# Two self-attentions of a decoder rebuilt around 32-row heads in fp32

## The chip, the cores and the metric

One core of a Trainium2 chip runs the whole program. The metric is the device time of one execution in microseconds (us); less is better. TensorE (PE) multiplies matrices, VectorE (DVE), ScalarE (ACT) and GpSimd (POOL) do elementwise work, and SyncE (SP) issues most DMAs. Results of TensorE land in PSUM, eight banks of 128 partitions by 512 fp32 numbers.

## What is computed

A decoder of four layers (attention, cross attention, feed-forward, each followed by a layer norm) on x of 2 x 1024 x 256. The change touches two of its attentions, both with 16 heads of width 16:

```python
# layer 1: causal
q = split_heads(x @ Wq + bq); k = split_heads(x @ Wk + bk); v = split_heads(x @ Wv + bv)
scores = einsum('bhqd,bhkd->bhqk', q, k) / sqrt(16)
scores = where(tril, scores, -10000.0)
ctx = softmax(scores) @ v;  return merge(ctx) @ Wo + bo
# layer 3: the last 64 keys, no biases
valid = (kpos >= qpos - 64 + 1) & (kpos <= qpos)
scores = einsum('bhqd,bhkd->bhqk', q, k) / sqrt(16) + where(valid, 0, -inf)
out = softmax(scores) @ v;  return merge(out) @ Wo.T
```

## The kernel before, in words

The stages run one after the other, each in blocks that end with all engines meeting. `attention` (line 775) makes the causal stage L1a and the window stage L3a. The 16 heads are cut into 4 units of 4 heads (HU = 4), for each of the 2 sequences: 8 units, in which every stage loops.

Each unit has two products of queries and keys. A **piece** has queries on the partitions and up to 512 keys in a row (`max_ps`, line 959), and VectorE takes its row maximum (`cmax`, line 1104). When a unit's 48 pieces (32 in the window stage) are done, VectorE negates and joins the maxima (`negc`), TensorE transposes them (`turn`, line 978), VectorE copies them (`crow`) and GpSimd's queue moves them by a DMA into one more row of the queries (line 938), so that the second product already has the maximum taken off. The **scores** (`st_ps`, line 997) have the keys on the partitions and up to 512 queries in a row; ScalarE takes exp of two heads at once (`prob`, line 1093). Then `values` multiplies prob by V with a column of ones (`acc`, line 1022); four heads go to four groups of 32 columns of the array. VectorE transposes acc, takes the reciprocal of the sums, multiplies, and transposes back into `o` (lines 1127 to 1141).

To be precise enough on TensorE's fp32r path, which takes one pass where fp32 takes two records of two passes each, the kernel splits queries and keys into a high and a low part. `project` makes them for all heads (lines 1034 and 1037), ScalarE writes the high part (line 1084), VectorE the low part (line 1164), SP stores them to memory (line 884) and loads them back four times stacked (lines 902, 907 and 910) as `qst` and `kst`, with 4 x 16 rows and one for the maximum. GpSimd first clears these buffers (lines 927 to 934). Masks are added by a second matmul with an identity (`identb`, lines 963, 966, 1000, 1003), for both products.

The order on TensorE is written out by hand: in the opening, all projections, with the first unit's pieces between the last of them; then per unit and step (12 in the causal stage, 8 tiles of 192 queries cut at the half in the window stage) scores of heads 0 and 1, scores of heads 2 and 3, and `values` of the step before, with the next unit's pieces dealt out at four spots of the step. Three banks hold pieces, so the next piece waits for the reduce of three pieces ago.

Two other stages serve the prediction as measures. `cross_attention` (line 1200) already keeps its heads in 32 rows each, of which 17 are used, in plain fp32 (line 1328 scores, line 1349 values, line 1291 projection). `paired_attention` (line 1507, stage L2a) runs two heads at a time in 64 rows each (line 1687 pieces, line 1701 scores, line 1716 values), with 16 steps per unit and three piece banks.

Of the kernel before, what the change touches and what calls it, by code (L numbers as in the profile page):

```python
# [5 lines left out]
F32 = mybir.dt.float32  # L6
# [29 lines left out]
STAGES = 7  # L36
# [723 lines left out]
def max_pieces(kind):  # L760

    out = []
    for t in range(S // P):
        if kind in ("full", "causal"):
            keys = S if kind == "full" else (t + 1) * P
            out += [(t, h, 1, k, min(CH, keys - k), k // CH) for h in range(HU) for k in range(0, keys, CH)]
        elif kind == "window":
            first = max(0, t * P - WIN)
            out += [(t, h, 2, first, (t + 1) * P - first, 0) for h in range(0, HU, 2)]
        else:  # L770
            out.append((t, 0, HU, 0, M, 0))
    return out


def attention(nc, env, dram, kind, scale, w_count, mask=None, ahead=None, masks=None):

    cross = kind in ("cross", "xcausal", "xmask")
    nk = M if cross else S
    nkp = M + 1 if cross else S
    kp = M if cross else P
    nkt = 1 if cross else S // P
    halves = S // CH
    steps = [(half, i == 0, i == len(steps_of(kind, half)) - 1, *t)
             for half in range(halves) for i, t in enumerate(steps_of(kind, half))]
    nsteps = len(steps)
    pieces = max_pieces(kind)  # L790
    NP = max(p[5] for p in pieces) + 1
    per_unit = len(pieces) + 1
    units = [(b, u) for b in range(NB) for u in range(NU)]
    piece_steps = {"full": range(0, nsteps - 1), "causal": range(0, nsteps - 2),
                   "window": range(2, nsteps - 3)}.get(kind, range(0, 2))
    turn_step = piece_steps[-1] + 1

    def pieces_at(i, spot):

        if i not in piece_steps:  # L800
            return range(0)
        n, i = 4 * len(piece_steps), 4 * piece_steps.index(i) + spot
        return range(i * len(pieces) // n, (i + 1) * len(pieces) // n)

    MAXB = 3
    RING = 4
    SLOTS = 4 if cross else 3
    LEAD = 2 if cross else 1
    items = []
    for b in range(NB):  # L810
        for m in range(KT):
            items += [(b, "q", m, c * CH, CH) for c in range(S // CH)]
# [2066 lines left out]
```

## Time and profile before

| | |
|---|---|
| median of 3 runs | 3301.66 us (3295.03 to 3303.44) |
| the profiled execution | 3299.8 us, span of its trace 3298.0 us |
| mean granted TensorE clock | 0.868 of 2.4 GHz |
| busy: PE, DVE, ACT, POOL | 2587.0, 1677.4, 1081.4, 759.1 us |
| costliest groups of L1a and L3a | reduce of pieces 268.6 us (line 1104), exp 211.7 (line 1093), matmuls of pieces 225.4 (line 959) and scores 203.1 (line 997), values 185.0 (line 1022) |

The busy sum of a group is the time in which at least one of its instructions runs; where four row tiles of the array work at once it is less than count times mean. Fp32 matmuls stand as two records each. A matmul's start is measured, its end modelled, so a cost per matmul is best read from one start to the next.

### The profile page before, as it was taken

Reading aid. Unit: us, or ns where it says so; the run is one execution under the profiler, and the core shown is the slowest. Engines: PE = TensorE matmul, PEld = TensorE weight load, DVE = VectorE, ACT = ScalarE, POOL = GpSimd, SP = SyncE. Lnnn points to the kernel's source line nnn. Section 1 sums busy time; section 2 is a strip of 40 time slices with the busy share of each in tenths; the row PEclk is TensorE's granted clock in tenths of the full one; section 3 lists DMA queues with packets and bytes.
Section 4 is the critical chain, followed back from the end, with each engine's and each line's share of the span. In section 5 each row is a group of like instructions: output and inputs, shape, how many; then the busy total and the mean of one; then the engine's idle time right before and its main releaser. Section 6 shows DMA issues by size and latency. Waiting matters only on the chain. (4 is left out here: it accounts for less than half of the span.)

```text
span 3298.0 us, 38083 instructions
## 1 busy us (share of the span) xinstructions
PE 2587.0 (78%) x14160; PEld 1667.8 (51%) x14160; DVE 1677.4 (51%) x3198; ACT 1081.4 (33%) x1858; POOL 759.1 (23%) x596
## 2 busy tenths in 40 slices
PE   0153089799999889996799898858889989589992
PEld 0143076444444357994333333336657753379992
DVE  6716963556645532224688874545635554441115
ACT  4212023234344321111165657331313333214441
POOL 7385903100000101332200000003140021025551
PEclk9956589899999889997898979868989999669996
DMA  3012103642300022994311110004186410139994
GB/s 129 15 62 87 53 1 84 112 52 33 46 1 21 2 103 71 332 332 145 58 20 29 30 20 7 2 10 129 44 183 79 53 36 2 50 131 353 353 346 184
DMA packets 92689, 313.41 MB, mean 95 GB/s; under 512 B 21279, under 2 KB 39991, under 8 KB 74194
## 3 DMA queue, kind: packets, MB, share of 16 engines
q1 hardware_dynamic: 76442, 276.93, 29.7%
q0 software_dynamic: 16064, 34.04, 3.3%
q8 instruction: 114, 1.87, 0.2%
q14 instruction: 69, 0.57, 0.1%
HBM read 258.74 MB, written 38.61 MB: 90 GB/s over the span
## 5 line engine op out<-in xcount | busy, mean ns | idle before, releaser
L1104 DVE TENSOR_REDUCE cmax<-max_ps 128x1 f32<-128x512 f32 (+5 forms) x512 | 268.6, 549 | 176.9 <-PE max_ps L963 71.2
L1808 DVE TENSOR_REDUCE cmax<-max_ps 128x1 f32<-128x512 f32 x512 | 318.6, 682 | 71.9 <-PE max_ps L1687 71.9
L1093 ACT ACTIVATE prob<-st_ps 128x1024 f32<-128x1024 f32 (+3 forms) x336 | 211.7, 652 | 372.4 <-PE st_ps L1000 171.4
L2428 PE MATMUL A<-xbT,w 128*128 128x128 f32 x2512 | 301.7, 276 | 2.3 <-DMA w<-L3f_W_dram 1.9
L2428 PEld LDWEIGHTS A<-xbT,w 128*128 128x128 f32 x2512 | 291.5, 193 | 3.4 <-DMA w<-L3f_W_dram 2.4
L1784 ACT ACTIVATE prob<-st_ps 128x1024 f32<-128x1024 f32 x256 | 247.1, 1021 | 140.2 <-PE st_ps L1701 140.2
L959 PE MATMUL max_ps<-kst,qst 128*128 128x192 f32 (+4 forms) x640 | 225.4, 397 | 25.2 <-DVE cmax L1104 13.1
L1687 PE MATMUL max_ps<-kst,qst 48*128 48x512 f32 x512 | 203.3, 504 | 41.1 <-DVE cmax L1808 21.0
L2439 PE MATMUL C<-w,hid 128*128 128x256 f32 x944 | 223.0, 380 | 0.0
L997 PE MATMUL st_ps<-qst,kst 128*128 128x512 f32 (+5 forms) x672 | 203.1, 378 | 20.1 <-DMA qst<-crow 17.4
L959 PEld LDWEIGHTS max_ps<-kst,qst 128*128 128x128 f32 x640 | 128.7, 205 | 143.0 <-DVE cmax L1104 102.5
L1687 PEld LDWEIGHTS max_ps<-kst,qst 48*128 48x128 f32 x512 | 88.3, 204 | 220.3 <-DVE cmax L1808 195.0
L2618 DVE COPY yb<-C 128x256 f32<-128x256 f32 x118 | 50.1, 424 | 283.4 <-PE C L2439 283.4
L2343 POOL DMA_INDIRECT y_rows_dram<-yb,dst x118 | 116.3, 986 | 330.5 <-DVE yb L2618 327.3
L1022 PE MATMUL acc<-prob,v 128*17 128x512 f32 (+5 forms) x1344 | 185.0, 419 | 0.7
L2439 PEld LDWEIGHTS C<-w,hid 128*128 128x128 f32 x944 | 170.6, 191 | 18.3
L2332 POOL DMA_INDIRECT xb<-x_rows_dram,src x118 | 115.4, 978 | 173.7 <-DVE dst L2593 138.4
L997 PEld LDWEIGHTS st_ps<-qst,kst 128*128 128x128 f32 x672 | 132.9, 206 | 41.6 <-DMA qst<-crow 20.1
L1716 PE MATMUL acc<-prob,v 128*17 128x512 f32 x1024 | 151.2, 666 | 0.4 <-ACT prob L1784 0.4
L1701 PE MATMUL st_ps<-qst,kst 49*128 49x512 f32 x512 | 140.2, 458 | 2.7 <-ACT prob L1784 2.7
L938 POOL DMA_DIRECT2D qst<-crow x16 | 8.4, 527 | 547.5 <-DVE crow L1118 547.5
L2499 ACT ACTIVATE hid<-A,w 128x128 f32<-128x128 f32 x316 | 90.1, 368 | 114.1 <-PE A L2428 114.1
(403 smaller groups left out, 4857.7 us busy)
## 6 DMA issues: line engine op xcount, KB each, us to landing
w<-L3f_W_dram SPq DMA_DIRECT2D x79, 1026.0 KB, 8.4
w<-L1f_W_dram SPq DMA_DIRECT2D x39, 1536.0 KB, 9.3
qst<-q_parts_dram SPq DMA_DIRECT2D x64, 256.0 KB, 9.5
kst<-k_parts_dram SPq DMA_DIRECT2D x64, 256.0 KB, 15.7
down_coef<-L0f_down_coef_dram SPq DMA_DIRECT2D x10, 1024.0 KB, 4.8
coef_u<-L0f_up_coef_dram SPq DMA_DIRECT2D x10, 1024.0 KB, 4.6
gate<-L2f_gates_dram SPq DMA_DIRECT2D x6, 1536.0 KB, 8.2
q_parts_dram<-o SPq DMA_DIRECT2D x16, 512.0 KB, 9.7
```

Of the source, the lines that this page charges most:

```text
L959: mm = pe.matmul(max_ps[:, g % MAXB, at:at + ne], qst[:, gu % SLOTS, h + a, t * P:(t + 1) * P], kst[:, gu % SLOTS, h + a, k0:k0 + ne], sta ...
L997: mm = pe.matmul(out, kst[:, gu % SLOTS, h, j * P:j * P + kp], qst[:, gu % SLOTS, h, lo:hi], start=True, stop=(not masked), skip_group_che ...
L1022: mm = pe.matmul(acc[32 * a:32 * a + HD + 1, lo - half * CH:hi - half * CH], v[:, b, j, u * HU + a, :], prob[:, g % 2, a, 0:hi - lo], star ...
L1093: act.activation(prob[:, g % 2, 2 * p:2 * p + 2, 0:hi - lo], st_ps[0:kp, p, :, 0:hi - lo], ACT.Exp, scale=scale).then_inc(s.exp_done, 1)
L1104: dve.tensor_reduce(cmax[:, h:h + nh, t, part], max_ps[:, g % MAXB, :].rearrange("p (a n) -> p a n", a=nh)[:, :, 0:n], AX.X, ALU.max).then ...
L1687: mm = pe.matmul(max_ps[:, e % MAXB, at:at + ne], qst[rows, gu % SLOTS, p, t * P:(t + 1) * P], kst[rows, gu % SLOTS, p, k0:k0 + ne], start ...
L1701: mm = pe.matmul(st_ps[0:kp, p, side, 0:hi - lo], kst[rows, gu % SLOTS, p, j * P:j * P + kp], qst[rows, gu % SLOTS, p, lo:hi], start=True, ...
L1716: mm = pe.matmul(acc[32 * a:32 * a + HD + 1, lo - half * CH:hi - half * CH], v[:, b, j, u * HU + a, :], prob[:, g % 2, a, 0:hi - lo], star ...
L1784: act.activation(prob[:, g % 2, 2 * p:2 * p + 2, 0:hi - lo], st_ps[0:kp, p, :, 0:hi - lo], ACT.Exp, scale=scale).then_inc(s.exp_done, 1)
L1808: dve.tensor_reduce(cmax[:, first:first + len(pairs), tiles[0]:tiles[0] + len(tiles), part], max_ps[:, e % MAXB, :].rearrange("p (a c n) - ...
L2428: mm = pe.matmul(A[:, j % 2 * 2 + a, f * TB:(f + 1) * TB], up_w(w[:, j % WB], a, k, f), xbT[:, j % 2, k, :], start=(k == 0), stop=(k == KT ...
L2439: mm = pe.matmul(C[:, j % 2, 0:D], hid[:, j % 2, f, 0:TB], down_w(w[:, j % WB], f), start=(f == 0), stop=(f == NF - 1))
```

## The change

Both stages go from `attention` to a new `self_attention`.

- Queries and keys are projected per unit and half of the sequence, in plain fp32, straight into `qT` and `kT`, in which head a of a unit has rows 32a to 32a+15 and row 32a+16 is the maximum (in kT a one). The weights come padded from the host and are loaded ahead, in the norm of the stage before (`more` and `w3`, two DMAs where there were three). The split into parts, the stores, the loads and the clearing are gone. Each unit has its own 4 projections (64 matmuls in all, as large as the 32 of before).
- The projections and V are no longer made in the opening, apart from the first unit's: they are dealt out after steps (`projections_due`).
- A **group** of matmuls takes scores of two heads and pieces of the two others, each in its own 32 rows. A step is group 0, `weigh` (the values) of two steps ago, group 1, and what is due. `weigh` issues its four heads without pieces between them.
- One ring of three PSUM banks serves pieces, turns, projections and V, in one order.
- The scores have no mask matmuls; GpSimd zeroes the masked part of prob with `affine_select` (line 932 of the new file), and `weigh` waits for that. The pieces keep theirs.
- Pieces lead by a whole unit (12 or 4 chunks), the maxima are turned per half unit, and SP issues four small DMAs for each turn. prob has three buffers.
- In the window stage a step joins two or three tiles of queries (4 steps per unit), a chunk two, and one reduce serves two tiles.

The core of the diff, new code only (in `group`, p is the group and c the chunk of pieces one unit ahead):

```python
                def group(step, p, c):
                    if pack:
                        g = step // nS
                        if step:
                            pe.wait_ge(s.exp_done, 2 * (step - 1) + p + 1)
                        if p == 0 and opens[step % nS]:
                            pe.wait_ge(c_loaded[half_of[step % nS]], 16 * HU * (g + 1))
...
                    for i in range(max(len(pack), len(chunk))):
                        if i < len(pack):
                            j, lo, hi, at = pack[i]
                            for side in range(2):
                                a = 2 * p + side
                                rows = slice(32 * a, 32 * a + HD + 1)
                                mm = pe.matmul(st_ps[:, p, side, at:at + hi - lo], kT[rows, g % SLOTS, j * P:(j + 1) * P],
                                               qT[rows, g % SLOTS, lo:hi], start=(i == 0), stop=True, skip_group_check=True)
...
                        if i < len(chunk):
                            t, k0, k1, at = chunk[i]
                            for side in range(2):
                                a = 2 * (1 - p) + side
                                key = ("piece", c, a)
                                if i == 0:
                                    room(key)
                                rows = slice(32 * a, 32 * a + HD)
                                mm = pe.matmul(spot(key)[:, at:at + k1 - k0], qT[rows, gm % SLOTS, t * P:(t + 1) * P],
                                               kT[rows, gm % SLOTS, k0:k1], start=(i == 0), stop=(not masked), skip_group_check=True)
...
                for step in range(NS):
                    c = step + LEAD if step + LEAD < NC else None
                    group(step, 0, c)
                    if step >= LAG:
                        weigh(step - LAG)
                    group(step, 1, c)
                    if c is not None:
                        extras(c)
```

`room(key)` waits until the holder of three ring entries ago is read. `extras` is the turn, if one is due, then the projections due: in the causal stage after chunks 0, 2, 4 and 7 of 12, in the window stage after 0 (two of them), 1 and 2 of 4.

```python
                for step in range(NS):
                    for i, (sign, base, c0, c1) in enumerate(masked_sides(step)):
                        if i:
                            pool.wait_ge(s.cleaned, cleaned_by[step] + i)
                        else:
                            pool.wait_ge(s.exp_done, 2 * (step + 1))
                        to = prob[:, step % PROBS, :, c0:c1]
                        pool.affine_select(out=to, in_=to, compare_op=ALU.is_ge, fill=0.0, base=base,
                                           pattern=[[0, HU], [sign, c1 - c0]], channel_multiplier=-sign).then_inc(s.cleaned, 1)
```

TensorE at the start of stage L1a, before: all projections (`w_1` are the weights; 1034 queries, 1037 keys, 1040 V), then the first pieces.

```order
L1034 MATMUL st_ps<-xT,w_1 128x512 x4
L1037 MATMUL st_ps<-xT,w_1 128x512 x4
L1034 MATMUL st_ps<-xT,w_1 128x512 x4
L1037 MATMUL st_ps<-xT,w_1 128x512 x4
L1040 MATMUL st_ps<-w_1,xT 128x256 x16
L1034 MATMUL st_ps<-xT,w_1 128x512 x4
L1037 MATMUL st_ps<-xT,w_1 128x512 x4
L1034 MATMUL st_ps<-xT,w_1 128x512 x4
L1037 MATMUL st_ps<-xT,w_1 128x512 x2
L959 MATMUL max_ps<-kst,qst 128x128
```

The same place now (952 is a projection of keys by `more` or queries by `w_1`, 962 of V, 998 pieces, 1006 their mask).

```order
L952 MATMUL ring<-xT,more 128x512 x2
L952 MATMUL ring<-xT,w_1 128x512 x2
L952 MATMUL ring<-xT,more 128x512 x2
L952 MATMUL ring<-xT,w_1 128x512 x2
L998 MATMUL ring<-kT,qT 128x512 x2
L1006 MATMUL ring<-causal_qk,identb 128x128 x2
L998 MATMUL ring<-kT,qT 128x512 x2
L1006 MATMUL ring<-causal_qk,identb 128x128 x2
L952 MATMUL ring<-xT,more 128x512 x2
L962 MATMUL ring<-w_1,xT 128x256 x4
```

The first piece now comes after 8 projecting matmuls and none of them has a trip through memory behind it; the rest of the projections has moved between the chunks.

TensorE in the middle of a causal unit, one step of 512 queries without a causal mask on the scores, before.

```order
L997 MATMUL st_ps<-qst,kst 128x512 x2
L959 MATMUL max_ps<-kst,qst 128x512
L997 MATMUL st_ps<-qst,kst 128x512 x2
L959 MATMUL max_ps<-kst,qst 128x256
L963 MATMUL max_ps<-causal_qk,identb 128x128
L1022 MATMUL acc<-prob,v 17x512 x2
L959 MATMUL max_ps<-kst,qst 128x512
L1022 MATMUL acc<-prob,v 17x512 x2
L959 MATMUL max_ps<-kst,qst 128x256
L963 MATMUL max_ps<-causal_qk,identb 128x128
```

And now (986 scores, 1045 the values in `weigh`), one step and the next one's start.

```order
L986 MATMUL st_ps<-qT,kT 128x512 x2
L998 MATMUL ring<-kT,qT 128x512 x2
L1045 MATMUL acc<-prob,v 17x512 x4
L986 MATMUL st_ps<-qT,kT 128x512 x2
L998 MATMUL ring<-kT,qT 128x512 x2
L986 MATMUL st_ps<-qT,kT 128x512 x2
L998 MATMUL ring<-kT,qT 128x512 x2
L1045 MATMUL acc<-prob,v 17x512 x4
```

Scores and pieces alternate in pairs, the values have become one run of four, and group 1 of a step stands right ahead of group 0 of the next.

GpSimd in the window stage, before: it clears the three slots of queries and keys, then issues a DMA per unit.

```order
L931 MEMSET kst 128x4096
L932 MEMSET qst 128x4096
L934 MEMSET kst 1x4096
L931 MEMSET kst 128x4096
L932 MEMSET qst 128x4096
```

And now: small clears, then the masking of prob, 17 instructions per unit (14 of 4 heads x 128 columns, 3 of 4 x 64).

```order
L921 MEMSET v 128x256
L922 MEMSET cmax 128x32
L932 AFFINE_SELECT prob<-prob 128x4x128 x7
L932 AFFINE_SELECT prob<-prob 128x4x64 x2
L932 AFFINE_SELECT prob<-prob 128x4x128 x7
L932 AFFINE_SELECT prob<-prob 128x4x64
```

The big clears of the opening have gone, and GpSimd works inside every step; in the causal stage it has 8 such instructions per unit, all of 4 x 128.

## Rows read from the trace of the kernel before

**Rows 1.** Windows: us, busy per engine (count), granted clock, DMA share, GB/s.

```profile
545.00:627.00 82.00, 63.22 (x209) 36.32 (x209) 41.58 (x83) 12.28 (x17) 40.76 (x15) 0.87 0.90 187
627.00:962.00 335.00, 322.46 (x1806) 156.07 (x1806) 204.71 (x398) 131.46 (x169) 13.50 (x21) 0.98 0.26 33
2390.00:2452.00 62.00, 53.97 (x193) 32.52 (x193) 26.72 (x51) 12.28 (x17) 38.64 (x14) 0.90 0.85 175
2452.00:2480.00 28.00, 22.57 (x116) 16.33 (x116) 5.72 (x11) 4.26 (x10) 0.59 (x1) 0.53 0.74 152
```

**Rows 2.** Timeline: start, length, engine, line; L1a's first matmul, first scores, first after it; L3a's end.

```profile
545.47 1.19 PE L1034 MATMUL st_ps<-xT,w 128*128 128x512 f32 x1 [1.77 <-PEq L2752]
...
627.34 0.79 PE L997 MATMUL st_ps<-qst,kst 128*128 128x512 f32 x1 [4.00 <-DMA qst<-crow]
...
989.18 3.39 PE L1193 MATMUL y_ps<-wo,o 128*128 128x256 f32 x8 [2.60 <-PEq L828]
...
2637.74 4.52 PE L1193 MATMUL y_ps<-wo,o 128*128 128x256 f32 x12 [2.60 <-PEq L828]
```

**Rows 3.** Sources: the DMA of each unit's maxima in L1a, in L3a, and L3a's first projections.

```profile
L938 POOL DMA_DIRECT2D qst<-crow x8: 501/507/766, 624.3 to 958.8; - x8
L938 POOL DMA_DIRECT2D qst<-crow x8: 496/497/591, 2452.1 to 2619.5; - x8
L1034 PE MATMUL st_ps<-xT,w x32: 592/592/1193, 2390.1 to 2423.6; 128*128 128x512 f32 x32
```

**Rows 4.** Timeline of TensorE in cross attention, clock 1.00: values, scores, projection; then a mask.

```profile
1062.64 1.05 PE L1349 MATMUL acc<-prob,v 77*17 77x512 f32 x8
1063.62 1.10 PE L1328 MATMUL st_ps<-qT,kT 17*77 17x512 f32 x8
1064.65 1.98 PE L1291 MATMUL pr_ps<-xT,wx 128*128 128x512 f32 x4
1066.47 2.56 PE L1307 MATMUL max_ps<-kbd,qT 128*128 128x308 f32 x8
...
1070.97 0.42 PE L1334 MATMUL st_ps<-causal_kq,identb 128*77 128x128 bf16 x4
1071.22 1.94 PE L1291 MATMUL pr_ps<-xT,wx 128*128 128x512 f32 x4
```

**Rows 5.** Timeline of TensorE in L1a: values in two halves, then in one run.

```profile
803.54 1.04 PE L1022 MATMUL acc<-prob,v 128*17 128x512 f32 x4
804.51 0.49 PE L959 MATMUL max_ps<-kst,qst 128*128 128x512 f32 x1
...
817.37 0.84 PE L1022 MATMUL acc<-prob,v 128*17 128x384 f32 x8
818.15 0.28 PE L978 MATMUL max_ps<-ident,negc 128*32 128x128 f32 x1
```

**Rows 6.** Groups by line and shape: busy us, mean ns; VectorE on pieces and on acc.

```profile
L1104 DVE TENSOR_REDUCE cmax<-max_ps 128x1 f32<-128x512 f32 x192 | 130.0, 687 | 59.9 <-PE max_ps L959 44.5 <-PE max_ps L963 14.7
L1104 DVE TENSOR_REDUCE cmax<-max_ps 128x2 f32<-128x384 f32 x112 | 60.5, 555 | 33.5 <-PE max_ps L966 33.2
L1127 DVE STREAM_TRANSPOSE w<-acc 128x512 f32<-128x512 f32 x32 | 22.9, 714 | 62.7 <-PE acc L1022 62.4
```

**Rows 7.** Timeline in the opening of L1a: from VectorE to TensorE to VectorE.

```profile
622.70 0.22 DVE L1113 TENSOR_REDUCE negc<-cmax 128x32 f32<-128x64 f32 x1
623.07 0.27 PE L978 MATMUL max_ps<-ident,negc 128*32 128x128 f32 x1 [1.56 <-DVE negc L1113]
623.37 0.28 DVE L1118 CAST crow<-max_ps 32x128 fp32r<-32x128 f32 x1 [0.45 <-PE max_ps L978]
```

**Rows 8.** Timeline of TensorE in L2a, two pairs abreast; then waits there, 1650 to 2000.

```profile
1732.67 0.40 PE L1687 MATMUL max_ps<-kst,qst 48*128 48x512 f32 x1
1732.68 0.62 PE L1701 MATMUL st_ps<-qst,kst 49*128 49x512 f32 x2
1733.38 0.49 PE L1687 MATMUL max_ps<-kst,qst 48*128 48x512 f32 x1
...
PEld max_ps L1687 <- DVE cmax L1808: 177.6, 218, 2.3
```

**Rows 9.** Groups by line and shape on GpSimd.

```profile
L133 POOL TENSOR_SCALAR_AFFINE_SELECT window_qk<-window_qk 128x192 bf16<-128x192 bf16 x1 | 0.4, 352 | 0.0
L116 POOL TENSOR_SCALAR_AFFINE_SELECT ident<-ident 128x128 f32<-128x128 f32 x1 | 0.3, 282 | 0.0
L288 POOL TENSOR_TENSOR down_tmp<-down_w,down_coef 128x1024 f32<-128x1024 f32 x20 | 56.4, 2842 | 80.4 <-DMA down_coef<-L0f_down_coef_dram 79.8
```

More of the change, by code:

```diff
@@ L775, in attention @@
[L775 to L792, printed above, removed]
-    units = [(b, u) for b in range(NB) for u in range(NU)]
[L794 to L812, printed above, removed]
-            items += [(b, "k", m, 0, M)] if cross else [(b, "k", m, c * CH, CH) for c in range(S // CH)]
-        items += [(b, "v", j, 0, 0) for j in range(nkt)]
-    early = [i for i, item in enumerate(items) if item[0] == 0]
-    later = range(len(early) + (1 if cross else 6), len(items))
-    opening = [("item", i) for i in range(later[0])]
-    for n, i in enumerate(later):
-        opening.append(("item", i))
-        opening += [("piece", p) for p in range(n * len(pieces) // len(later), (n + 1) * len(pieces) // len(later))]
-    qk_items = [i for i, item in enumerate(items) if item[1] != "v"]
@@ L1010, in values, with room @@
[L1010 to L1024 removed]
+                def room(key):
+                    e = entries[key][0]
+                    if e >= RING:
+                        pe.wait_ge(*freed(e - RING))
@@ new lines, in project @@
+                def project(what, g, half):
+                    key = (what, g, half)
+                    b, u = units[g]
+                    room(key)
+                    w = wk if what == "keys" else wq
+                    for k in range(KT):
+                        mm = pe.matmul(spot(key), w[:, k, u * P:(u + 1) * P], env.xT[:, k, b * S + half * CH:b * S + (half + 1) * CH],
+                                       start=(k == 0), stop=(k == KT - 1), skip_group_check=True)
+                    mm.then_inc(s.act_filled, 1)
@@ new lines, in project_values @@
+                def project_values(b, x):
+                    key = ("values", b, x)
+                    room(key)
+                    for i in range(2):
+                        tok = b * S + (2 * x + i) * P
+                        for k in range(KT):
+                            mm = pe.matmul(spot(key)[:, i * D:(i + 1) * D], env.xT[:, k, tok:tok + P], wv[:, k, :],
+                                           start=(i == 0 and k == 0), stop=(k == KT - 1), skip_group_check=True)
+                    mm.then_inc(s.dve_filled if biased else s.act_filled, 1)
@@ L1168, in _ @@
[L1168 to L1189 removed]
+                dve.wait_ge(s.max_cleared, 1)
```

700 lines of the change are left out of this document (353 added, 347 removed).

## The prediction

> **What bounds the kernel now.** I read the windows first, to find the two stages on the time axis and how full TensorE is in each part of them. L1a runs from its first projection at 545.5 to the first matmul after it at 989.2, 443.7 us; L3a from 2390.1 to 2637.7, 247.6 us [rows 2, 3]. Each has an opening with holes, then a full stretch. The opening of L1a takes 82 us, with TensorE busy for 63 and the DMA engines 90% busy on the trip through memory; its last wait is 4 us for the maxima [rows 1, 2]. In L3a the maxima of the first unit leave at 2452.1, 62 us after the start, and the next 28 us run at a granted clock of 0.53 [rows 1, 3]. After that TensorE is 96% busy (322 of 335 us), VectorE 61%, ScalarE 39% [rows 1]. So in the steady part the order on TensorE sets the time. Its beat is the interval between the DMAs of the maxima, seven of them in 334.5 us, 47.8 us a unit in L1a; 167.4 us, 23.9 a unit, in L3a [rows 3].
>
> **Costs, at the full clock.** Cross attention has the new form already. Four heads in 32 rows each, 512 columns, take 1.03 us from start to start; the values of four heads 0.98; two full projecting matmuls of 512, 1.82; four mask matmuls of 128 columns 0.25, so two cost 0.13 [rows 4]. With 384 columns the values take 0.78 [rows 5], 0.2 less for 128 columns. I scale groups alike: 1.03, 0.82, 0.61, 0.39 for 512 to 128 columns, values 0.98, 0.78, 0.56, 0.34.
> A group here mixes scores and pieces with 128 output rows, where the rows have one kind and 77; L2a shows pieces and scores starting together in two row tiles [rows 8]. I take 1.03, with 1.03 + 0.86 (two pairs in turn) as the other end.
> The reduce of 512 columns takes 0.69 us, of 2 x 192 0.56 [rows 6]. From the end of a VectorE instruction to TensorE's start is 0.15 [rows 7], and I add 0.15 for the way there.
> For `affine_select` over 4 x 128 the near rows are 0.28 us for 128 columns and 0.35 for 192; the slope gives 0.67 for 512. The other end is the two-input operation, 2.84 for 1024, so about 1.45. I take 0.67, from the same instruction [rows 9].
>
> **The opening.** Parts, stores, loads and clearing go. Left are four projections, 4 x 1.8, and 1.0 until ScalarE has kept the last: 8.2 us. Then the first unit's pieces run alone, two heads per group. In a masked chunk the second piece of a group waits for the first reduce of the group before (0.69 + 0.3), runs 0.96, and is masked (0.15): 2.1 us per group at 512, or 4.2, 3.5, 2.8, 2.1 us per chunk by width, 12.6 for four, twice; the four unmasked ones go by VectorE at 2.5 each: 35. The projections and V due there, eight of about 1.8, are half hidden behind reduces, +13, and the turn 1. Opening of L1a: 57 us, where it was 82. In L3a the chunks are four at 3.6, the projections 16: 8 + 14 + 16 = 38, where it was 62 and the 6 until the maxima had landed, in part at half clock.
>
> **The steady part of L1a.** TensorE's own work per unit: 24 groups 19.6 us, 16 mask pairs 2.4, values 9.3, four projections 7.2 (a cost that was in the opening, and doubled), two turns 0.4: 38.9. The values save most: before, two heads at a time cost 0.97 [rows 5], so 1.94 per 512 columns and not 0.98.
> But group 1 stands right before the next group 0, and the ring has three banks. The fourth matmul of group 0 needs the bank of group 1's first piece: 0.15 + 0.69 + 0.15 = 1.0 us after group 1 ends. By then its three partners are nearly done, so group 0 lasts 1.0 + 0.95 = 1.95 instead of 1.03, and `weigh` and group 1 queue behind. A step of 512 columns is thus 1.95 + 0.98 + 1.03 = 3.96. L2a shows this wait: the fourth comes 0.70 after the third, and there weight loads wait 218 times, 177.6 us in all, for the reduce [rows 8]. A projection between the two covers it and costs 0.9 net; with a turn before it, which takes a bank, the projection itself waits 1.0.
> Step by step (each with the values of two steps before, masks and what is due): 6.6, 2.8, 5.1, 1.9, 6.0, 3.0, 3.95, 5.8, 3.3, 3.8, 3.3, 2.5, which is 47.9 us a unit where it was 47.8. What the values save the waits and projections eat. VectorE has 48 reduces (26 us) and some 5 us of transposes [rows 6], 31 in all, and ScalarE 22, under that.
> Six units at 47.9, the seventh without projections 43.2, the last without pieces 28, V for the second sequence 7, the tail 2.5, and 0.8 a unit for small waits of engines on each other (before: 1.8 a unit, of which 1.0 was the wait for the maxima, [rows 1]) over seven, 5.6: 373.9. With the opening 431, so **L1a gains 12**.
>
> **The steady part of L3a.** Group 0 with two tiles: 0.65 until the fourth may start, 0.64 for two pieces, masks of 384 columns twice 0.2, in all 1.8; group 1 1.22 to 1.38; values 0.83 to 1.2. Steps 8.5, 5.1, 6.2, 3.3 with their projections (three in four steps, since two stand after one): 23.1 us a unit, where it was 23.9 with the slow stretch in it. Six of them 138.6, then 16.5, then 14 (there GpSimd's 17 masks at 0.67 + 0.15 count), V 7.3, tail and small waits 8, opening 38.5: 223. **L3a gains 25.** The wait for GpSimd in a whole unit costs nothing: exp and 4 masks are done 4.2 us after a step, `weigh` comes 5.6 after it.
>
> **The sum.** 3299.8 - 12.3 - 24.6, plus 4 for stretches of half clock in the new openings (projections and pairs at 1.2 GHz; a guess within the 13 us that the 28 us at 0.53 lost before, [rows 1]), plus 2.6 for two more meetings of all engines: 3269.5. The profiled execution lies 1.9 below the median, within the spread; a change under 0.3%, 10 us, can't be told from none.
>
> **A rule against a row.** The row says four tiles in 1.03 us, against 4 x 0.86 one by one, 3.3 times as fast [rows 4]. The Trainium skill, "TensorE: Matmul & The Clock Gate", Part 3 (measured speedup), has 3.07 for four row tiles of 512 columns. By it a group would be 1.12, some 1.6 us more per causal and 0.5 per window unit, 17 us in all, and the time would be an estimated 3287. I go by the row.
>
> **The rivals.**
> *The ring never waits* (12%). If the reduce is done sooner than I reckon, or the four tiles make up the lag, a causal unit is 39 us and a window unit 22: 7 x 9 + 7 x 1 = 70 less, 3200. For it: VectorE has a third of the time free. Against it: L2a's waits [rows 8].
> *GpSimd sets the pace of L3a* (12%). At 1.45 us a mask, 17 masks and hand-overs are 25.3 us a unit: 6 x 2.2 + 8.8 + 11.3 = 33 more, 3303, no change. In L1a 8 masks, 13 us, stay hidden. It decides from about 1.3 us a mask. For it: no row has this shape. Against it: the two rows of the same instruction [rows 9].
> The Trainium skill, "GPSIMD Engine Reference", section 3.1, has 769 ns for a one-input loop over 512 elements; by this price a window unit of GpSimd would be an estimated 15 us, and the sum the same.
> *The groups don't run four abreast* (12%), which is the case on the other side. If scores and pieces of one group take turns as pairs, each group costs up to 0.86 more per 512 columns: 15.4 us a causal unit, of which 5 lie in the waits anyway, and 3.5 a window unit: 7 x 10.4 + 7 x 3.5 = 97 more, 3367. It turns the result when a third of the groups does so. For it: the two kinds read different tiles and write more rows. Against it: [rows 4, 8].
> The rest (8%) is small waits at twice my size, both ways.
>
> **How the numbers follow.** My forecast holds 56%, 3270 with its own range of 3245 to 3295. The range of 8 in 10 reaches to the fast rival's near part and over the GpSimd case: 3212 to 3315; outside are the slow rival and half of the fast one. Faster by over 0.3% is nearly all of the forecast, the fast rival and a little of the rest: 0.70; within 0.3%: the edge of the forecast and most of the GpSimd case, 0.12; slower: the slow rival and tails, 0.18.
>
> **What would show it.** Right: the first scores of L1a some 57 us after its start, the turns of full units 48 us apart, and between group 1 and the next group 0 a fourth matmul that comes 1.0 us late, with the reduce named as what it waits for; in L3a first scores after 38 us and 23 us a unit. A fast rival shows units of 39 and TensorE without these waits; the GpSimd case shows `weigh` waiting for masks of over 1.3 us; the slow one groups of 1.9 us with no wait in them. The prediction is wrong where the openings stay above 70 us, or the clock in the row-tiled stretches falls below 1.00.

## The result, and the profile after

The changed kernel is slower: 3391.62 us median (3386.10 to 3396.84) beside 3298.35 for the kernel before, ratio 1.028 with a 95% interval of 1.0256 to 1.0313. The prediction was 3270 with a range up to 3315. The profiled execution spans 3391.9 us. The stages, cut at the same instructions as in [rows 2], show where it went:

| stage | before | after | difference | predicted |
|---|---|---|---|---|
| L1a, causal attention (changed) | 443.7 | 543.4 | +99.7 | -12 |
| L2a, full attention (code unchanged) | 491.7 | 507.1 | +15.4 | 0 |
| L3a, window attention (changed) | 247.6 | 226.3 | -21.3 | -25 |
| everything else | 2115.0 | 2115.1 | 0 | +2.6 |

The cuts of the profile after, from its timeline of TensorE (start, length, engine, line, operation); they answer [rows 2] and the last row of [rows 3]:

```profile
543.82 1.19 PE L952 MATMUL ring<-xT,more 128*128 128x512 f32 x1 [1.77 <-PEq L2779]
...
1087.17 1.19 PE L1211 MATMUL y_ps<-wo,o 128*128 128x256 f32 x2 [2.60 <-PEq L866]
...
2507.28 1.19 PE L952 MATMUL ring<-xT,more 128*128 128x512 f32 x1 [1.35 <-PEq L2787]
...
2733.63 1.19 PE L1211 MATMUL y_ps<-wo,o 128*128 128x256 f32 x2 [2.60 <-PEq L866]
```

The windows of the changed kernel show where the time goes. They are, in this order, L1a's opening and rest, a good stretch and the last stretch of that rest, L2a, and L3a's opening and rest. After the busy times stands the granted clock of TensorE as a share of 2.4 GHz, so that 0.50 is its lower level of 1.2 GHz. The counts in brackets are records, two for each fp32 matmul:

```profile
core 0: us, PE busy (x) PEld busy (x) DVE busy (x) ACT busy (x) POOL busy (x), PEclk, DMA share, GB/s
543.80:613.60 69.80, 68.67 (x193) 32.43 (x193) 27.75 (x53) 6.78 (x9) 0.58 (x2) 0.77 0.03 8
613.60:1087.20 473.60, 460.85 (x2577) 159.72 (x2576) 204.07 (x428) 170.15 (x217) 51.64 (x80) 0.74 0.00 1
640.00:700.00 60.00, 58.02 (x397) 23.79 (x396) 32.01 (x69) 25.03 (x32) 8.47 (x13) 1.00 0.01 1
981.00:1087.00 106.00, 101.55 (x477) 30.21 (x476) 30.07 (x64) 34.94 (x45) 12.26 (x19) 0.50 0.00 1
1656.20:2163.30 507.10, 450.57 (x2184) 172.87 (x2185) 360.48 (x601) 265.64 (x290) 47.77 (x79) 0.84 0.15 27
2507.30:2548.00 40.70, 39.37 (x149) 21.86 (x149) 8.00 (x22) 9.17 (x13) 0.52 (x2) 0.85 0.03 7
2548.00:2733.60 185.60, 173.68 (x1884) 95.92 (x1884) 88.01 (x228) 68.81 (x93) 82.03 (x136) 0.92 0.01 2
```

The rest of L1a runs at 0.74, where the kernel before had 0.98 in its steady part [rows 1]. It isn't one slow stretch: the clock is 1.00 from 640 to 700 us, then falls to 0.50 and comes back once or twice per unit, and from 981 to the end it stays at 0.50. TensorE is 97% busy all the while (460.85 of 473.60), so it isn't idleness that takes the clock away. In L2a, whose code is the same, it is 0.84 after and was 0.88 before. The same two windows of the kernel before, L1a from its first scores to its end, and L2a:

```profile
627.00:989.00 362.00, 345.93 (x1975) 166.64 (x1975) 208.92 (x406) 149.76 (x192) 13.50 (x21) 0.98 0.24 30
1554.80:2046.50 491.70, 435.35 (x2184) 167.04 (x2184) 360.03 (x601) 265.58 (x290) 47.77 (x79) 0.88 0.16 27
```

The timeline of TensorE in one unit shows both levels. In these rows, first the values and groups while the clock is low, then a projection, then the same values and groups when it is back:

```profile
835.45 1.91 PE L1045 MATMUL acc<-prob,v 128*17 128x512 f32 x8
837.29 1.22 PE L986 MATMUL st_ps<-qT,kT 17*128 17x512 f32 x2
837.30 1.22 PE L998 MATMUL ring<-kT,qT 16*128 16x512 f32 x2
838.31 1.06 PE L986 MATMUL st_ps<-qT,kT 17*128 17x512 f32 x2
838.32 1.06 PE L998 MATMUL ring<-kT,qT 16*128 16x512 f32 x2
839.31 3.78 PE L952 MATMUL ring<-xT,w 128*128 128x512 f32 x4
...
844.65 1.05 PE L1045 MATMUL acc<-prob,v 128*17 128x512 f32 x8
845.63 0.70 PE L986 MATMUL st_ps<-qT,kT 17*128 17x512 f32 x2
845.64 0.70 PE L998 MATMUL ring<-kT,qT 16*128 16x512 f32 x2
846.16 0.59 PE L986 MATMUL st_ps<-qT,kT 17*128 17x512 f32 x2
846.18 0.59 PE L998 MATMUL ring<-kT,qT 16*128 16x512 f32 x2
846.71 0.28 PE L1006 MATMUL ring<-causal_qk,identb 128*128 128x128 bf16 x2
```

At the upper level a group of four row tiles takes 1.08 us (845.63 to 846.71), where the sum had 1.03, and the values 0.98 (844.65 to 845.63), where it had 0.98. At the lower level the group takes 2.02 (837.29 to 839.31) and the values 1.84. So the durations of the prediction hold at 2.4 GHz, within 0.05 us a group; what failed is the assumption that the kernel would be allowed to run there. In the groups 17 or 16 of the 32 rows of each row tile are in use, 66 of 128 rows in all; before, each matmul of pieces and scores read 128 rows (lines 959 and 997 slice no rows), 4 x 16 of them with parts, one with the maximum and the rest cleared to zero. (The expectation of e1 says 68; it is 2 x 17 + 2 x 16 = 66.)

### The profile page after: what moved, and what is told of

Same layout as the page of the kernel before. It is cut to its first block and busy times, and to the rows that moved or that the text cites. A ratio compares the mean times of both kernels' runs of the same rounds, so it can differ in the third digit from the quotient of the medians.

```text
span 3391.9 us, 40148 instructions
## 1 busy us (share of the span) xinstructions
PE 2704.4 (80%) x14976; PEld 1612.5 (48%) x14976; DVE 1638.3 (48%) x3206; ACT 1099.9 (32%) x1818; POOL 797.0 (23%) x758
## 5 line engine op out<-in xcount | busy, mean ns | idle before, releaser
L998 PE MATMUL ring<-kT,qT 16*128 16x192 f32 (+4 forms) x1280 | 336.9, 529 | 3.1 <-ACT qT L1078 1.6
L1128 DVE TENSOR_REDUCE cmax<-ring 128x1 f32<-128x512 f32 (+3 forms) x416 | 205.2, 530 | 237.3 <-PE ring L1006 169.0
L1107 ACT ACTIVATE prob<-st_ps 128x1024 f32<-128x1024 f32 (+5 forms) x256 | 203.9, 803 | 322.0 <-PE st_ps L986 319.9
L986 PE MATMUL st_ps<-qT,kT 17*128 17x512 f32 (+5 forms) x1344 | 279.0, 542 | 1.5 <-ACT prob L1107 1.0
L932 POOL TENSOR_SCALAR_AFFINE_SELECT prob<-prob 128x512 f32<-128x512 f32 (+1 forms) x200 | 122.6, 614 | 627.7 <-ACT prob L1107 620.6
L986 PEld LDWEIGHTS st_ps<-qT,kT 17*128 17x128 f32 x1344 | 117.5, 219 | 145.3 <-issue 106.9
L998 PEld LDWEIGHTS ring<-kT,qT 16*128 16x128 f32 x1280 | 146.9, 208 | 53.7 <-DVE cmax L1128 31.5
L1045 PE MATMUL acc<-prob,v 128*17 128x512 f32 (+5 forms) x1344 | 138.5, 513 | 3.2 <-POOL prob L932 3.2
```

Source lines behind the costliest of these rows:

```text
L986: mm = pe.matmul(st_ps[:, p, side, at:at + hi - lo], kT[rows, g % SLOTS, j * P:(j + 1) * P], qT[rows, g % SLOTS, lo:hi], start=(i == 0), s ...
L998: mm = pe.matmul(spot(key)[:, at:at + k1 - k0], qT[rows, gm % SLOTS, t * P:(t + 1) * P], kT[rows, gm % SLOTS, k0:k1], start=(i == 0), stop ...
L1045: mm = pe.matmul(acc[32 * a:32 * a + HD + 1, lo - half * CH:hi - half * CH], v[:, b, j, u * HU + a, :], prob[:, step % PROBS, a, at:at + h ...
L1107: act.activation(prob[:, step % PROBS, 2 * p:2 * p + 2, 0:n], st_ps[:, p, :, 0:n], ACT.Exp, scale=scale)\
L1128: dve.tensor_reduce(cmax[:, a, t:t + 1, part(k0)], spot(key)[:, 0:k1 - k0], AX.X, ALU.max)\
```

## The experiments

**Four theories.** A: the clock falls where few of the array's rows are in use. B: it falls because of the wait for a ring bank, after which the fourth matmul of a group runs alone. C: what held it up was work on the whole array at once, which the old code had more of and which row tiles can't replace. D: the episodes are chance of phase.

**e1_rows32**: the row slices of scores and pieces alone.

```
-   rows = slice(32 * a, 32 * a + HD + 1)      # scores
+   rows = slice(32 * a, 32 * a + 32)
-   rows = slice(32 * a, 32 * a + HD)          # pieces
+   rows = slice(32 * a, 32 * a + 32)
```

> The changed kernel, with one edit: the score matmuls and the piece matmuls (the products whose maxima give each query's shift) read all 32 rows of their row tile instead of 17 and 16; rows 17 to 31 hold zeros, and so does row 16 of the queries while the pieces run, so the products are the same. A matmul of the changed kernel passes one column per cycle whatever its rows, so the nominal work is unchanged. Causal attention of layer 1 took 543.4 us in the changed kernel, of which the prediction had 431; its granted clock alternates between 1.00 and 0.50 from 704 us on, and is 0.50 throughout from 981 to 1092. Theory A (the clock falls where few rows of the array are in use: 68 of 128 in a group): with 128 of 128 rows the granted clock stays 1.00 up to the values, layer 1's stage falls to 435 to 450 us, the total to 3285 to 3300, and the 15 us that layer 2's windowed attention lost come back at best too (3275). Theory B (the fourth matmul of a group runs alone after a wait for a ring bank, so the array is thinly used): unchanged, 3392 within 10. Theory C (what keeps the clock up is work on the whole array, 128 rows and 128 columns, which the old causal code had more of): unchanged, 3392 within 10, since a row tile still makes its product on its own 32 rows. Theory D (the episodes are chance of phase): a few of them move, 3380 to 3400.

Measured: 3280.48 us, ratio to the kernel before 0.993 (0.990 to 0.9957), 111 us under the changed kernel; the profiled execution took 3294.7, 14 above the median. L1a takes 444.4 us and L3a 217.9. The windows of this kernel: L1a's opening and its rest, L3a's opening and its rest, a stretch of L1a's opening, and L2a:

```profile
546.10:613.70 67.60, 66.49 (x196) 32.01 (x196) 27.87 (x54) 6.78 (x9) 0.52 (x2) 0.78 0.04 8
613.70:990.50 376.80, 363.53 (x2577) 134.92 (x2576) 203.02 (x428) 169.26 (x217) 51.63 (x80) 0.99 0.01 1
2418.00:2455.50 37.50, 36.17 (x152) 20.15 (x152) 8.06 (x22) 9.17 (x13) 0.54 (x2) 0.93 0.03 8
2455.50:2635.90 180.40, 166.34 (x1884) 92.47 (x1883) 87.86 (x228) 68.81 (x92) 81.89 (x136) 0.97 0.01 2
583.00:597.00 14.00, 14.00 (x31) 6.03 (x30) 8.70 (x13) 0.00 (x0) 0.00 (x0) 0.65 0.00 0
1556.70:2074.30 517.60, 461.32 (x2184) 178.56 (x2185) 360.55 (x601) 265.59 (x290) 47.76 (x79) 0.81 0.15 26
```

The same 2577 records take 376.8 us instead of 473.6, and the clock is 0.99 instead of 0.74. Cut into steps of 10 us, it is 1.00 in every step from 625 to 985 us. The added rows hold zeros, in the keys too but for a one that meets a zero of the queries, so it is rows read that count here, not what stands in them. Theory A's stage came in (435 to 450); its total (3285 to 3300) did in the profiled execution, and the median is 5 us lower. B, C and D had expected little or no change. C falls in the form in which I put it: no full-array work was added, and the clock came back. D falls too: no episode is left after 625, nor is there one in the same stretch of e5 and e9 below. B falls as a cause by itself, because the wait that it blames is still there (total us, times, longest us; the changed kernel has 30.5 in 63, shown further down):

```profile
PEld ring L998 <- DVE cmax L1128: 34.5, 73, 1.0
```

In the changed kernel the clock does fall beside such waits, at 703.9 us and within 3 us of the one at 828.3, so they may have a part in when it falls; with all rows read it stays up through all of them. What is left over is the opening, still at 0.78, and L2a, at 517.6 us.

**e3_split_values**: the values of two heads after group 0, of the other two after group 1.

```
     group(step, 0, c)
     if step >= LAG:
-        weigh(step - LAG)
+        weigh(step - LAG, (0, 1))
     group(step, 1, c)
+    if step >= LAG:
+        weigh(step - LAG, (2, 3))
```

> The changed kernel, with one edit: the four value matmuls of a step are no longer in one run after its first group of four row tiles, but two after the first group and two after the second. Now the wait for a ring bank that stood ahead of the last row tile of the second group has two value matmuls (0.48 us at full clock) more of other work behind it. At full clock the unit is the same within 1 us: the value work is moved, not added. Theory B (a fourth matmul that runs alone behind a ring wait is what thins the array and halves the clock): the granted clock rises over most of 704 to 981 us and layer 1's causal stage falls from 543 to 440 to 480 us, total 3290 to 3330. Theories A (too few rows of each tile) and C (too little work on the whole array): the same instructions in the same amounts, so the stage stays within 15 us of 543 and the total in 3375 to 3405. If the run of values was itself what held the clock up, splitting it could lengthen the half-clock stretches: up to 3420.

Measured: 3505.56 us, ratio 1.063 (1.0571 to 1.0694). L3a takes 271.8 us at a clock of 0.83, and L1a 610.9 at 0.77, where the changed kernel had 0.74 over the whole stage. Theory B's rise over most of the stage is missing. But the kernel lost another 114 us, far outside what any theory said, and the mistake was mine. Two runs of values in its timeline, at the upper clock level:

```profile
740.67 1.04 PE L1045 MATMUL acc<-prob,v 128*17 128x512 f32 x4
741.64 0.70 PE L986 MATMUL st_ps<-qT,kT 17*128 17x512 f32 x2
...
742.93 1.04 PE L1045 MATMUL acc<-prob,v 128*17 128x512 f32 x4
```

Two heads (x4) take 0.97 us, as long as four (x8) took above: the four value matmuls run abreast in four column tiles, and split in two runs they cost twice. The prediction had used just this for the changed kernel (its 0.98 against 1.94), and I forgot it in the experiment. Nor did the split take away what B blames: TensorE still waits for a bank ahead of pieces, 27.8 us in 39 weight loads and 9.7 us in 14 matmuls, beside 30.5 in 63 and 0.5 in 2. So e3 tests nothing, neither by its time nor by its clock; what speaks against B is e1.

**e4_filler**: more work on all 128 rows.

```
+   if pack:
+       wide = pack[-1][3] + pack[-1][2] - pack[-1][1]
+       for side in range(2):
+           mm = pe.matmul(st_ps[:, p, side, 0:wide], env.identb[:, :], nought[:, 0:wide], start=False, stop=True, ...)
+       mm.then_inc(s.s_ready, 1)
```

> The changed kernel with work added: behind each group of scores two more matmuls of the identity (128 rows, 128 columns) with zeros are added onto the scores' banks, as wide as the group, which changes nothing in the result. At full clock they cost 2 times 512 columns at 2.4 GHz, 0.43 us on a group of 1.03, some 9 us on a unit of 47.8 and some 70 us on layer 1's causal attention, some 35 us on layer 3's. Theory C (work on the whole array keeps the clock at its upper level): the granted clock of layer 1's steady part is 1.00, the stage takes 431 + 70 = about 500 us, 40 us less than the 543 of the changed kernel although it has more to do, and layer 3's rises from 226 to about 260; total 3370 to 3400, with the granted clock telling the verdict, not the time. Theories A and B: the clock falls as before and the added work is paid at the half rate as well: stage 600 to 640 us, total 3480 to 3530. Theory D: somewhere between, with the half-clock stretches at other places.

Measured: 3390.49 us, ratio 1.029 (1.0211 to 1.0363), level with the changed kernel although it does more. The windows are L1a's opening, its rest, and L3a:

```profile
544.00:613.60 69.60, 68.45 (x193) 32.41 (x193) 27.75 (x53) 6.78 (x9) 1.06 (x3) 0.77 0.03 8
613.60:1081.80 468.20, 453.59 (x2931) 166.01 (x2960) 206.50 (x428) 172.25 (x217) 51.77 (x80) 0.91 0.01 1
2488.70:2726.20 237.50, 224.25 (x2161) 125.50 (x2161) 98.39 (x249) 78.31 (x106) 83.46 (x139) 0.97 0.01 3
```

The clock rose from 0.74 to 0.91, and where nothing was added, in the opening, it stayed at 0.77. Neither account on record fits: C has the total (3370 to 3400), but it wanted 1.00 and 500 us in L1a (which took 537.7), and A and B wanted no rise. I had put A wrongly there, since matmuls on 128 rows raise the rows in use as well. With e1 the two agree: rows in use can be had by wider slices for nothing, or by added matmuls that cost time.

**e2_old_causal**: L0 to L2 as before, the new form in L3a alone.

> The kernel before, with only layer 3's windowed attention in the new form (unit by unit, four row tiles per group), and layers 0, 1 and 2 as they were. It asks whether the two halves of the change add up. Layer 3's stage went from 247.6 to 226.3 us in the changed kernel; what layer 2 lost (491.7 to 507.1 us) stands in code that the change doesn't touch. If layer 2's loss came from the disturbed layer 1 ahead of it, it is gone here, and the total is 3298 - 21 + 2 = 3279 (range 3270 to 3288), faster than the kernel before. If the loss belongs to the new code of layer 3 (its weights' loads run during layer 2) it stays: 3294. If layer 3's granted clock depends on what went ahead, its stage is back at 240 or more: 3290 to 3310.

Measured: 3280.99 us, ratio 0.995 (0.9924 to 0.9984), as in the first case on record (3279). L3a takes 226.4 us, as in the changed kernel, L1a 441.7, L2a 487.9 against 491.7. So the window half of the change holds its gain by itself, and L2a's loss is gone when L1a is the old one. But e1, with a sound L1a, has L2a at 517.6, so it wasn't L1a's low clock that carried over; see e5.

**e6_rows24 and e7_pieces32**: how much of it is needed, and where.

> The changed kernel with 24 rows read in each row tile by both scores and pieces, between its own 17 and 16 (3392 us) and the 32 of e1_rows32 (3280). It asks for the shape of the dependence. If every row adds its share (linear): 24 lies half way, about 3335, layer 1's stage near 494. If there is a level from which the clock holds: 24 gives either all of the gain (3275 to 3290, stage near 444, clock 0.99 in its steady part) or nearly none (3370 to 3392). I take the level as likelier, and 24 of 32 as just above it, since the values and projections already use all 128 rows: 3290.

> The changed kernel with 32 rows in the piece matmuls alone; the scores keep their 17. The last unit of layer 1's stage has scores and values but no pieces, and was wholly at 0.50 in the changed kernel. If the rows in use count together, a group holds 2 tiles of 32 rows and 2 of 17, 98 of 128, much like 24 in each (96), so this run lands within 15 us of e6_rows24, and only the last unit (28 us at full clock, about twice that at half) stays slow: 3290 to 3320. If only one of the two kinds of matmul matters, it is within 10 us of 3392 or of 3280.

Measured: 3307.40 us with 24 rows in both kinds, ratio 1.0026 (1.0002 to 1.005), L1a 467.0; 3322.61 with 32 in the pieces and 17 in the scores, ratio 1.0054 (1.0015 to 1.0092), L1a 487.3. Two windows of the first, L1a's rest, and in it the stretch from the last projection to the last piece:

```profile
613.60:1012.80 399.20, 386.08 (x2586) 140.71 (x2584) 203.74 (x430) 169.51 (x217) 51.84 (x80) 0.93 0.01 1
915.30:972.10 56.80, 56.67 (x434) 20.51 (x432) 34.62 (x74) 24.95 (x32) 8.39 (x13) 1.00 0.01 2
```

Three windows of the second, up to 926 us, from there to the last piece, and to the end of L1a:

```profile
612.50:926.00 313.50, 305.16 (x2083) 114.43 (x2083) 171.97 (x362) 134.57 (x171) 39.39 (x61) 0.97 0.01 1
926.00:984.00 58.00, 58.00 (x283) 19.42 (x281) 25.06 (x51) 16.20 (x20) 5.18 (x8) 0.53 0.00 1
984.00:1032.10 48.10, 43.42 (x218) 11.01 (x212) 6.58 (x15) 18.82 (x26) 7.09 (x11) 0.51 0.00 1
```

With 17 and 16, 24 and 32 rows per tile L1a took 543.4, 467.0 and 444.4 us: 24 rows gave 77% of the stage's gain, neither the half of a straight line nor all of it, and the total is 17 us above the 3290 that I had put on record. With 32 rows in the pieces alone the total fell by 69 of the 111 us of e1, so each kind of matmul has its share.

Where the clock falls in e7 is not where I had expected it. It goes at 926 us, after the last projection (906.0), and the 32-row pieces run on at 0.53 until 984; so it isn't only the last unit, without pieces, that is slow. The changed kernel shows the same order: last projection at 958.8, 0.50 from 981, last piece at 1038.7. Here e6 differs, with nearly the same sum of rows (96 in a group, 98 in e7): its clock stays at 1.00 through the same work, and falls only behind the last piece. So the sum of rows over a group doesn't order the two by itself. This rests on one execution of each, and e7's is the longest of its ten, 3338.0 us beside 3286.5 to 3337.8 for the others. No run here settles it.

**e5_rows64**: e1, and the same in L2a, two row tiles of 64 rows with 49 and 48 in use.

```
-   rows = slice(64 * side, 64 * side + HP)        # pieces
+   rows = slice(64 * side, 64 * side + 64)
-   rows = slice(64 * side, 64 * side + HP + 1)    # scores
+   rows = slice(64 * side, 64 * side + 64)
+   for at in (0, 64):                             # in stack_q: row 48 is zeroed
+       eng.dma_start(qst[at + HP:at + HP + 1, g % SLOTS, :, :].bitcast(F32),
+                     qst[at + HP + 1:at + HP + 2, g % SLOTS, :, :].bitcast(F32)).then_inc(stacked[g % SLOTS], 16)
```

> The kernel of e1_rows32 with the same edit in layer 2's full attention, whose score and piece matmuls run in row tiles of 64 rows with 49 and 48 of them in use: they read all 64. Rows 49 to 63 hold zeros in the queries; row 48, which holds the shifts of an earlier unit, is zeroed by two small DMAs per unit ahead of the pieces. Layer 2's stage took 491.7 us in the kernel before, 507.1 in the changed one, 517.6 in e1_rows32, with the same work and a granted clock that falls to 0.50 at changing places, some 90 to 150 us in all. If rows in use set the clock, as e1 showed for layer 1, the stage's steady part runs at 1.00 and the stage takes 445 to 470 us, total 3215 to 3245. If 48 of 64 rows was already enough and these episodes have another cause (the projections and their gaps, the DMA trip of the parts), the stage stays at 488 to 518 and the total at 3270 to 3290. The two DMAs per unit (0.5 us each on SP's queue, beside others) cost nothing that TensorE waits for in the first case and at most 1 us per unit, 8 us, if it does.

Measured: 3254.01 us, ratio 0.986 (0.981 to 0.9906): 1.4% under the kernel before, and 4% under the changed one. L2a's window:

```profile
1558.80:2031.10 472.30, 414.19 (x2184) 158.39 (x2185) 359.90 (x601) 266.35 (x290) 47.76 (x79) 0.93 0.17 29
```

472.3 us at 0.93. That is less gain than expected (445 to 470); short dips remain, and a low stretch near its start, in which TensorE has next to nothing to do (busy for 2.0 of the 15 us from 1573.8). Put beside the other profiled executions it shows L2a's share: with 48 and 49 rows it took 487.9 to 517.6 us in eight kernels (before 491.7, after 507.1, e1 517.6, e2 487.9, e3 502.6, e4 494.6, e6 509.8, e7 515.2), with all 64 rows 472.3, 480.3 (e8), 480.3 and 480.0 (e9, e10). The +15.4 of the changed kernel lies inside the spread of the first eight. L1a took 449.2 us in this execution, 444.4 in e1's, with the same code.

**e8_old_causal_rows**: e2 with all rows read in L2a and L3a.

> The kernel of e2_old_causal (layer 1 as before, layer 3 in the new form; 3281 us) with all rows read in layer 3's row tiles and in layer 2's, as in e1 and e5. Layer 1's stage stays at 442 to 444 us; layer 3's falls from 226 to 218, as in e1; layer 2's by what e5 shows. Against e5_rows64 it tells whether the new or the old causal code is the better one once the clock holds: the two stages measured 444.4 (e1) and 441.7 (e2), so this one is level with e5 or up to 5 us faster: 3210 to 3245 if layer 2 gains, 3262 to 3275 if it doesn't.

Measured: 3260.39 us, ratio 0.987 (0.9815 to 0.992); L1a 446.6, L2a 480.3, L3a 218.0. It can't be told from e5, and lies above the 3210 to 3245 on record, as e5 does. With the clock held in its steady part, the new causal code (444.4 and 449.2) is as fast as the old one (441.7 and 446.6) and no faster; e9 changes that a little.

**e9_opening**: e5, with score-shaped matmuls on the two row tiles that are idle while the first unit's pieces run alone.

```
+   if not pack:
+       t, k0, k1, at = chunk[i]
+       for side in range(2):
+           rows = slice(32 * (2 * p + side), 32 * (2 * p + side) + 32)
+           pe.matmul(st_ps[:, p, side, at:at + k1 - k0], qT[rows, ...], kT[rows, ..., k0:k1], start=(i == 0), stop=True, ...)
```

> The kernel of e5_rows64 with matmuls added in the openings of layers 1 and 3 alone: while the first unit's pieces run, only two of the four row tiles are at work (64 of 128 rows), and the granted clock is 0.78 over the 67 us of layer 1's opening, 0.50 in the run of pieces from 588 to 597 us. Each such group gets two more score-shaped matmuls on the other two row tiles, whose results nothing reads; a group of four costs 1.03 us against 0.95 to 1.13 for two at full clock, so they are nearly free. If rows in use set the clock here too, the opening's clock goes to 0.90 or more and it takes 57 to 61 us instead of 67.6 (my prediction had 57), layer 3's 34 to 37 instead of 39, and the total falls by 8 to 12 from 3254: 3242 to 3248. If the openings' low clock comes from their short waits and switches between kinds of work, they stay at 66 to 70 us, total 3252 to 3262.

Measured: 3252.76 us, ratio 0.984 (0.9811 to 0.9876). The windows of L1a's opening and rest:

```profile
544.90:603.50 58.60, 57.79 (x292) 29.26 (x292) 27.62 (x54) 6.78 (x9) 0.55 (x2) 0.97 0.03 10
603.50:982.20 378.70, 365.57 (x2577) 135.44 (x2576) 202.99 (x428) 169.27 (x217) 51.68 (x80) 0.99 0.01 1
```

There are 48 matmuls more (some 100 records), and the opening is 9 to 11 us shorter: 58.6 instead of 67.6 in e1 and 69.3 in e5, since the clock in it is 0.97 instead of 0.78 and 0.77. The stage took 437.3, after 444.4 in e1 and 449.2 in e5 (437.7 in e10, which has the same edit). L3a's opening, 37.6 us, is no shorter than e1's 37.5. The total didn't show the gain, 3252.8 against 3254.0, and misses the 3242 to 3248 on record: L2a took 480.3 in this execution and 472.3 in e5's.

**e10_cross**: e9, and all 32 rows in the cross attentions' scores (17 and 9 before).

> The kernel of e9_opening with the scores of the cross attentions reading all 32 rows of their row tiles too (17 or 9 until now; the rest holds zeros). Their granted clock in e5_rows64 was 0.91 over 156 us in layer 1, 0.80 over 152 us in layer 2 (with 9 rows) and 0.86 to 0.92 in layer 3, and the pieces there already use the whole array. If rows in use in the scores are what is missing, layer 2's cross attention loses up to 152 x 0.1 = 15 us and the three together 10 to 20; but TensorE is busy for only 116 of layer 2's 152 us, and a low clock behind waits can't be mended so: then within 5 us of e9_opening. I take the second as likelier.

Measured: 3248.70 us, ratio 0.984 (0.9808 to 0.9868), within 5 us of e9, as I had thought likelier. Layer 2's cross attention went from 153.0 to 150.8 us; there TensorE waits too much of the time for this to matter. It is the fastest of the kernels here, though not measurably faster than e5 or e9.

## Why the prediction was wrong

The step that failed is in the sum: "plus 4 for stretches of half clock in the new openings". It granted half clock to the openings alone and took the steady part at the full one, because the kernel before ran there at 0.98 [rows 1]. That clock belonged to the old operands with their 128 rows, and the change replaced them with 16 and 17 rows per tile. The rows that I costed the groups from, cross attention's [rows 4], were taken in a stretch at 1.00 and said nothing on how long it lasts with this work alone. The last sentence of the prediction named the sign, "or the clock in the row-tiled stretches falls below 1.00", and I gave it neither a rival nor a chance.

How much each step was off:

- *L1a's steady part.* Predicted 373.9 us, measured 473.6, and 376.8 in e1, 379.9 in e5 and 378.7 in e9, where the clock is 0.98 to 0.99. The working is right within 2% at the clock that it assumed, and the clock cost 97 us. A unit, predicted 47.9, is 48.8 in e1 and 58.4 in the changed kernel, by VectorE's copies of the maxima, first two of e1 and then two of after:

```profile
789.30 0.27 DVE L1152 COPY crow<-ring 16x128 f32<-16x128 f32 x1
...
838.13 0.27 DVE L1152 COPY crow<-ring 16x128 f32<-16x128 f32 x1
```

```profile
880.92 0.27 DVE L1152 COPY crow<-ring 16x128 f32<-16x128 f32 x1
...
939.27 0.27 DVE L1152 COPY crow<-ring 16x128 f32<-16x128 f32 x1
```

- *L1a's opening.* Predicted 57, plus the guess of 4 for both openings; measured 69.8 at a clock of 0.77. e9 took 58.6 at 0.97. Here too the working holds, and the term for the clock was too small.
- *L3a.* Predicted 223, measured 226.3; opening 38 against 40.7. This stage masks 384 columns with matmuls on the whole array in every chunk and projects twice as often per time, and its clock stayed at 0.92; with all rows read it took 217.9 (e1) and 221.4 (e5).
- *The ring.* It waits as predicted, and the rival without waits (3200) is out. The waits of TensorE's queue in the changed L1a (total us, times, longest us), and the fourth piece of a group in the timeline, 0.66 us after the last matmul beside it:

```profile
PEld ring L998 <- DVE cmax L1128: 30.5, 63, 1.0
```

```profile
827.40 0.59 PE L998 MATMUL ring<-kT,qT 16*128 16x512 f32 x1
827.66 0.58 PE L986 MATMUL st_ps<-qT,kT 17*128 17x512 f32 x1
828.32 1.12 PE L998 MATMUL ring<-kT,qT 16*128 16x512 f32 x2
```

- *GpSimd.* Predicted 0.67 us a mask, with 1.45 as the other end [rows 9]; the rival at 3303 is out. The groups of the changed kernel by shape:

```profile
L932 POOL TENSOR_SCALAR_AFFINE_SELECT prob<-prob 128x512 f32<-128x512 f32 x176 | 112.7, 641 | 601.0 <-ACT prob L1107 595.0
L932 POOL TENSOR_SCALAR_AFFINE_SELECT prob<-prob 128x256 f32<-128x256 f32 x24 | 9.9, 414 | 26.7 <-ACT prob L1107 25.6
```

- *Groups not four abreast* (3367) came nearest in time and is wrong in kind: a group takes 1.08 us at the upper clock and 2.02 at the lower. Without the clock's column the second number would have passed for this rival.
- *The rule of 3.07.* The Trainium skill, "TensorE: Matmul & The Clock Gate", Part 3 (measured speedup), has this figure for four row tiles. Four single matmuls of 0.86 in 1.08 us are 3.2 times as fast. The 0.86 isn't in [rows 4], which have 1.82 for two; it is two projecting matmuls in 1.72 us at another place of the trace before (1022.64 to 1024.36). The skill's figure and my 1.03 lie on either side, and the 17 us between them decided nothing.
- *Slips of adding.* The twelve steps of a unit add up to 48.05 and not 47.9, the steady part to 373.7 and not 373.9, and 443.7 less 431 is 12.7 and not the 12.3 of the sum. Together they are under 2 us.
- *L2a* had no term. Its time moves by 30 us from kernel to kernel with unchanged code, so a change elsewhere of under some 15 us can't be read from the total of one execution of this program.

The Trainium skill, "TensorE: Matmul & The Clock Gate", Part 1, says that the array's default is throttled "and activity releases the throttle", and its section on oscillation asks for no long idle gaps of TensorE. The windows agree with it so far: the clock has two levels, 0.50 and 1.00, and it is low where TensorE stands idle (0.58 over the 15 us of e5's L2a in which it was busy for 2.0). But in the changed kernel TensorE was 97% busy with the clock at 0.74, and in e1 96% busy (363.5 of 376.8) with the clock at 0.99: being busy wasn't enough here, and the rows in use made the difference.

What stays open: which property of a matmul the chip counts (rows alone, or rows times something else) wasn't measured, nor why e6 and e7 differ once the projections are over, nor why L2a's episodes fall differently from one kernel to the next, nor whether two low stretches that are left in L2a's opening can be mended as in e9.

## What to carry to other kernels

Where a change packs small matmuls into row tiles, let each read all the rows of its tile, with zeros in the spare ones: it costs no time at a given clock (at 1.00 the two halves of a group start 0.53 us apart with 16 and 17 rows and with 32) and was worth 111 us of 3392 here. A forecast from durations must carry the granted clock as a term of its own, and ask of each new stretch how many rows its matmuls use, not only how busy TensorE is. When the durations of a trace are twice the expected ones, look at the clock's column before looking for a lost overlap.

## What the runs showed of the hardware

- With 66 of 128 rows in use and TensorE 97% busy the granted clock was 0.74 over 474 us, and 0.50 for the last 106 us without a break; with 128 rows, the added ones holding zeros, 0.99 over 377 us.
- 24 rows per tile gave 0.93 over the same work. 32 rows in the pieces and 17 in the scores gave 0.97 as long as projections ran between them, and 0.53 over the next 58 us of pieces, scores and values without projections (one execution).
- In row tiles of 64 rows, L2a took 487.9 to 517.6 us at a clock of 0.81 to 0.89 with 48 and 49 rows read, and 472.3 to 480.3 at 0.91 to 0.93 with all 64.
- Matmuls added on idle row tiles made an opening shorter: 58.6 us with them, 67.6 and 69.3 without.
- Four value matmuls in four column tiles take 0.98 us, and two of them 0.97.
- `affine_select` over 128x512 took 0.641 us, over 128x256 0.414.
